# Loads, statistics and three operations in another order at the seams of a time-mixing stage

## The reference, cut to what matters

```
xn  = layernorm(x);  sx = shift(xn) - xn                      # previous row, the state's for the first
xxx = tanh((xn + sx * maa_x) @ maa_w1);  five corrections = xxx_j @ maa_w2_j
x5_j = xn + sx * (maa_stack_j + correction_j)                 # decay, key, value, receptance, gate
w = exp(-exp(time_decay + tanh(x5_w @ decay_w1) @ decay_w2))
r, k, v = x5_r @ Wr.T, x5_k @ Wk.T, x5_v @ Wv.T;  g = silu(x5_g @ Wg.T)
s <- k v + w * s  for each of 128 rows, out = r . (u * k v + s)   # a 16 x 16 state for each of 32 heads
x = x + (groupnorm(out) * g) @ Wo.T
```

## Time and profile before

| | |
|---|---|
| median of three runs | 3070.8 us |
| the profiled execution | 3071.39 us, its span 3069.6 us |
| time mixing ends, channel mixing begins (first instruction of DVE) | 751.41 us |
| PE, DVE, ACT, POOL busy, share of the span | 94%, 58%, 38%, 17% |
| granted TensorE clock, mean | 0.973 |

### The profile page before, as it was taken

One profiled execution on the slowest core, in us unless ns is written; L12 is line 12 of the kernel. 1 busy time (PEld: TensorE's weight loads), 2 busy tenths in 40 slices (PEclk: granted clock), 3 DMA queues, 4 the chain that ended last, 5 costly groups with the idle time before them and its releaser, 6 DMA issues.

```text
span 3069.6 us, 41094 instructions
## 1 busy us (share of the span) xinstructions
PE 2881.2 (94%) x14864; PEld 2179.8 (71%) x14864; DVE 1779.6 (58%) x2615; ACT 1163.7 (38%) x2537; POOL 534.8 (17%) x375
## 2 busy tenths in 40 slices
PE   5988889896897999999999999999999999999899
PEld 2333333332776888888888878888888888888787
DVE  5988979796866444455444464454444554444644
ACT  3232323221534343434434343354434453433432
POOL 2856747483001000001000010010000000000100
PEclk8989999997998999999999999999999999999999
DMA  5001010102124111110111112121110111111011
GB/s 159 1 13 43 1 56 0 42 0 73 67 80 159 55 38 55 38 55 32 38 55 38 55 35 62 41 90 38 55 38 31 55 39 55 38 49 33 22 55 55
DMA packets 54779, 148.71 MB, mean 48 GB/s; under 512 B 6256, under 2 KB 7536, under 8 KB 53584
## 3 DMA queue, kind: packets, MB, share of 16 engines
q1 hardware_dynamic: 51824, 143.80, 14.1%
q0 software_dynamic: 2880, 3.94, 0.6%
HBM read 131.20 MB, written 12.58 MB: 47 GB/s over the span
## 4 chain that ended last, share of the span: by engine, by line
PE 67%; DVE 2%; ACT 1%; issue 0%; DMA 0%; ACTq 0%; DVEq 0%
PE ca_ps L60 19%; PE ca_ps L62 19%; PE ca_ps L61 19%; PE ca_ps L1954 4%; PE ca_ps L1938 4%; PE ca_ps L1946 2%; PE ca_ps L1980 1%; DVE ca_stats L68 0%; DVE ca_xres L1715 0%; DVE ca_ctx_lo L1746 0%; DMA ca_xres<-in_ctxT 0%; DVE ca_wq_lo L1673 0%; ACT ca_sk L1631 0%; DVE ca_h_lo L1740 0%; ACT L1631 0%
## 5 line engine op out<-in xcount | busy, mean ns | idle before, releaser
L1715 DVE TENSOR_TENSOR ca_xres<-ca_xres,ca_ps 128x512 f32<-128x512 f32 x384 | 264.1, 688 | 243.8 <-PE ca_ps L62 238.9
L1502 ACT ACTIVATE ca_pr<-ca_ps,ca_nb 128x129 f32<-128x129 f32 x512 | 181.8, 368 | 511.0 <-DVE ca_nb L1698 510.9
L60 PE MATMUL ca_ps<-ca_h_hi,ca_wq_hi 128*128 128x512 f32 x768 | 312.7, 407 | 4.7 <-DVE ca_h_lo L1740 4.2
L609 DVE TENSOR_TENSOR_SCAN tm_xn<-tm_wd,tm_vb 128x512 f32<-128x512 f32 x256 | 298.5, 1208 | 12.0 <-POOL tm_xf L316 3.5
L62 PE MATMUL ca_ps<-ca_h_hi,ca_wq_lo 128*128 128x512 f32 x768 | 302.6, 394 | 0.0
L61 PE MATMUL ca_ps<-ca_h_lo,ca_wq_hi 128*128 128x512 f32 x768 | 300.6, 391 | 0.0
L60 PE MATMUL ca_ps<-ca_wv_hi,ca_ctx_hi 128*128 128x256 f32 x1024 | 298.0, 291 | 0.0
L62 PE MATMUL ca_ps<-ca_wv_hi,ca_ctx_lo 128*128 128x256 f32 x1024 | 287.6, 281 | 0.0
L61 PE MATMUL ca_ps<-ca_wv_lo,ca_ctx_hi 128*128 128x256 f32 x1024 | 287.3, 281 | 0.0
L1455 POOL TENSOR_TENSOR ca_dv<-ca_bvr 128x256 f32<-128x256 f32 x32 | 23.8, 745 | 1453.9 <-DVE ca_v L1683 1443.8
L60 PE MATMUL ca_ps<-ca_wo_hi,ca_ct_hi 128*128 128x512 f32 x640 | 253.5, 396 | 0.2 <-DVE ca_xres L1715 0.2
(11 more groups left out here) (232 smaller groups left out, 5799.6 us busy)
## 6 DMA issues: line engine op xcount, KB each, us to landing
ca_sq<-in_wq SPq DMA_DIRECT2D x49, 512.0 KB, 5.2
ca_so<-in_wo SPq DMA_DIRECT2D x48, 512.0 KB, 3.5
ca_sk<-in_wk SPq DMA_DIRECT2D x33, 512.0 KB, 6.5
ca_sv<-in_wv SPq DMA_DIRECT2D x32, 512.0 KB, 3.7
ca_bvr<-in_bvb SPq DMA_DIRECT2D x32, 256.0 KB, 3.9
tm_xq<-in_x SPq DMA_DIRECT2D x16, 256.0 KB, 4.5
tm_xres<-in_x SPq DMA_DIRECT2D x4, 1024.0 KB, 6.1
x_dram<-tm_xres SPq DMA_DIRECT2D x4, 1024.0 KB, 4.7
```

The costliest lines, as they stand in the source:

```text
L60: pe.matmul(out, lhs[0], rhs[0], start=first, stop=False)
L609: v.tensor_tensor_scan(state[t % 2][:, d, :], wd[:, g].rearrange("p b t -> p (b t)"), pair[:, d, :], 0.0, ALU.mult, ALU.add).then_inc(scan ...
L1502: ins = act.activation(pr[hd][:, b, :], ps[:, BANK_SC + b // 2, o:o + KW], ACT.Exp, bias=nbs[hd][:, b:b + 1], scale=SCALE, accum_out=sms[h ...
L1715: v.tensor_tensor(xres[U.h][:, U.quad * 4 + b, :], xres[U.h][:, U.quad * 4 + b, :], ps[:, BANK_O + b % 2, :], ALU.add).then_inc(o_out, 1)
```

## The change

- **SP.** The loop is written out. The rows of quad q + 2 and the states of quad q + 1 are requested in the turn of quad q, after its `xres` and ahead of the wait for `res_added`. Quad 1's rows are still requested at the start.
- **DVE, statistics.** `norm_stats` and `norm_gather` for quads 2 and 3 go from between the mixes of `body(1)` and `body(2)` into `joint(0)` and `joint(1)`: two ahead of `gated(q, 2)`, two and the gather behind `inverse(q, 3)`. Quad 1's stay in `body(0)`.
- **DVE, wait.** The wait for PE's last accumulation (`rs_used`) moves from ahead of `shift` to behind its first small copy.
- **DVE, mix.** `mix(q + 1, 1, 0)` goes ahead of `hidden_lo_last`.
- **DVE, loop.** Quads 1 and 2 are written out instead of looped.
- **ACT.** `gate_mix(1)` goes ahead of `decay(2)`.
- **PE.** `value(0)` waits for `decay_out` 5 instead of 8: for `decay(2)` to have read its bank, not for all decays.

```diff
@@ SP
+            load_states(0)
+            ... (wk, wr)
+            load_rows(1)
+            ... (wg, wo)
+            for q in range(NQ):
                 sp.wait_ge(x2_out, q * 16 + 16)
                 sp.dma_start(xres[:], ...).then_inc(res_in, 16)
+                if q < NQ - 2:
+                    load_rows(q + 2)          # waits for xn0_ready, (q + 2) * 4
+                if q < NQ - 1:
+                    load_states(q + 1)        # waits for s0_set, (q + 1) * STEPS
                 sp.wait_ge(res_added, q * 4 + 4)
                 sp.dma_start(x2[...], xres[:]).then_inc(x2_out, 16)
-            quad(0, True, False)
-            with sp.Fori(1, NQ - 1) as q:
-                quad(q, False, False)
-            quad(NQ - 1, False, True)
@@ ACT body
                 gate_mix(0)
+                gate_mix(1)
                 decay(2)
                 decay(3)
-                gate_mix(1)
@@ DVE shift
                 v.wait_ge(sx_ready, q * 5 + 1)
+                if q > 0:
+                    v.wait_ge(rs_used, q * STEPS)
@@ DVE body
                     mix(q, 4, c, first)
-                    if not last:
+                    if first:
                         norm_stats(q + 1, c)
-                if not last:
+                if first:
                     norm_gather(q + 1)
@@ DVE joint
+                more = q + 2 < NQ
+                if more:
+                    norm_stats(q + 2, 0)
+                    norm_stats(q + 2, 1)
                 gated(q, 2)
                 v.wait_ge(rs_ready, q * STEPS + STEPS)
-                v.wait_ge(rs_used, q * STEPS + STEPS)
                 shift(q + 1)
                 inverse(q, 3)
+                if more:
+                    norm_stats(q + 2, 2)
+                    norm_stats(q + 2, 3)
+                    norm_gather(q + 2)
                 hidden_lo(q + 1)
                 gated(q, 3)
+                mix(q + 1, 1, 0)
                 hidden_lo_last(q + 1)
-                mixes(q + 1, 1)
+                for c in range(1, EC):
+                    mix(q + 1, 1, c)
@@ DVE
-            with v.Fori(1, NQ - 1) as q:
+            for q in range(1, NQ - 1):
                 body(q, False)
                 joint(q)
@@ PE value
-                            pe.wait_ge(decay_out, q * 8 + 8)
+                            pe.wait_ge(decay_out, q * 8 + 5)
```

More of the change, by code:

```diff
@@ L220, in _, with load_rows, load_states @@
                 sp.dma_start(tile[:], io[name]).then_inc(const_in, 16)
-            def quad(q, first, last):
-                if not first:
+            def load_rows(q):
+                sp.wait_ge(xn0_ready, q * 4)
+                for b in range(4):
+                    load_x(q, b)
+            def load_states(q):
+                if q > 0:
                     sp.wait_ge(s0_set, q * STEPS)
                 sp.dma_start(s0[:], io["s0"][bass.ds(q, 1)].rearrange("a p c d b -> (a p) c d b")).then_inc(s0_in, 16)
-                if first:
-                    sp.dma_start(wk[:], io["l0w"][1]).then_inc(wkr_in, 16)
-                    sp.dma_start(wr[:], io["l0w"][2]).then_inc(wkr_in, 16)
-                if not last:
[L230 to L235, removed]
+            load_states(0)
+            sp.dma_start(wk[:], io["l0w"][1]).then_inc(wkr_in, 16)
+            sp.dma_start(wr[:], io["l0w"][2]).then_inc(wkr_in, 16)
+            load_rows(1)
+            sp.dma_start(wg[:], io["l0w"][3]).then_inc(late_in, 16)
+            sp.dma_start(wo[:], io["l0w"][4]).then_inc(late_in, 16)
+            for q in range(NQ):
                 sp.wait_ge(x2_out, q * 16 + 16)
                 sp.dma_start(xres[:], io["x"][bass.ds(q * 4, 4)].rearrange("b t e -> t b e")).then_inc(res_in, 16)
+                if q < NQ - 2:
+                    load_rows(q + 2)
+                if q < NQ - 1:
+                    load_states(q + 1)
                 sp.wait_ge(res_added, q * 4 + 4)
                 sp.dma_start(x2[bass.ds(q * 4, 4)].rearrange("b t e -> t b e"), xres[:]).then_inc(x2_out, 16)
-            quad(0, True, False)
-            with sp.Fori(1, NQ - 1) as q:
-                quad(q, False, False)
-            quad(NQ - 1, False, True)
             sp.wait_ge(x2_out, NQ * 16 + 16)
```

## The result

The changed kernel takes 3050.9 us (median of four executions, 3048.88 to 3053.72) against 3069.84 for the kernel before; the ratio is 0.9943, with a 95% interval of 0.9930 to 0.9955. On record was 3051.5, between 3045 and 3060. The profiled execution took 3048.88, with a span of 3047.1: 22.5 less than the span of 3069.6. It is the fastest of the four, and the profile before (3071.39) lies near that kernel's slowest; the medians differ by 19.0. What follows explains the 22.5.

The account below looks back on a forecast made before the run. DVE's instructions bound time mixing's steps, chained waits its joints, PE the rest. Gains of 21.2 less 0.9 and 0.3, plus 1.5 for a vanished low stretch, minus 1.5 for clock: 20.0 off 3071.4; forecast 3051.5 us, range 3045 to 3060.

Parts of the forecast that it names:

- Part 1: First two joints: rows requested early and statistics moved into DVE's waits, at no cost there; gain 10.8 us.
- Part 2: gate_mix(1) ahead of decay(2) ends PE's stop ahead of mix(5, 2): 6.5 us over three joints, 3.0 in the opening.
- The 1.5 of the vanished low stretch: First joint: low clock following PE's stop ahead of mix(5, 2) should go with the stop, gaining 1.5 us.
- Part 3: mix(1, 0) ahead of hidden_lo_last, where DVE waits for ACT's copy: 0.3 us a joint, 0.9 in all.
- Part 4: Wait for rs_used behind shift's copy: 0, since the slowed subtraction would end with POOL's addition anyway; otherwise 0.9 us.
- Part 5: DVE's quads 1 and 2 written out: steps lose 0.9 us, double waits in two joints 0.3.
- Part 6: PE's low clock may fall inside any joint: 1.5 us lost, bounds -3.1 (first spared) and +6.2 (both others hit).
- the order moves the stop only: Rival: PE's stop moves to mix(3, 3) or mix(4, 0), gaining 2 or 3 instead of 11; 3060 us, chance 0.09.
- the stall stays: Rival: receptance(0) again runs at low clock, so DVE's wait for POOL's first product stays; 3055 us, chance 0.07.
- The clock lands in both later joints: Rival: the low clock falls into the second and third joints; 3056 us, chance 0.17.
- Better than I say: Rival: the first joint is spared the low clock as well; 3047 us, chance 0.12.
- slower: Rival: low clock settles in the dense steps, each microsecond costing up to 0.8; some 3080 us, chance 0.02.

Follow-up runs that it names:

- b_gate: Kernel before with one part alone, ScalarE's gate_mix(1) ahead of decay(2): 3064.45 us against 3068.27, ratio 0.9989.
- u_gate: Changed kernel with ScalarE's gate_mix(1) back behind decay(3): 3065.04 us.
- u_decay: Changed kernel with value(0) waiting for all eight decay outputs again: 3055.15 us.
- u_rs: Changed kernel with DVE's wait for rs_used back ahead of the copy that opens shift: 3049.6 us.
- c_loop: Changed kernel with DVE's quads 1 and 2 in a loop again, and statistics taken once more that nothing reads: 3050.32 us.
- m_first: Changed kernel with DVE's wait for rs_ready moved from the scan to the product ahead of it: 3052.76 us.
- b_loads: Kernel before with SyncE's new order alone (rows and states requested early): 3069.02 us against 3069.48, ratio 1.0000.
- w_warm: Changed kernel with four throwaway TensorE products, one at each of t = 27 to 30 of every quad: 3048.76 us.
- w_fill: Changed kernel with six throwaway TensorE products in every quad, two at t = 26, one at each of t = 27 to 30: 3048.66 us.
- c_both: Changed kernel with DVE's quads 1 and 2 looped again and six throwaway TensorE products (t = 26 to 30) in every quad: 3049.99 us.

## Why the prediction was right, step by step

The mechanisms of parts 1 and 2, which make most of the gain, came out as told; that the total was off by only 0.6 is in part luck. The 20.0 was taken off the profile's 3071.4 although that is 0.6 above the median; off the median it gives 3050.8. Between the medians the gain was 19.0, 1.0 less than 20.0, and between the profiles, to which the terms below add up, 22.5, 2.5 more. Single terms were off by up to 2.3, in both directions.

- **Part 1, 10.8: right.** 11.05 - 5.96 = 5.09 and 11.71 - 5.96 = 5.75, 10.84. By the runs the early rows are 2.5 + 3.2 and the statistics 2.4 each, 10.5 of the 10.8. "Both are covered, the first by 0.1 only" held.
- **Part 2, 6.5 in the joints and 3.0 in the opening: right in mechanism, small in size.** b_gate and u_gate give 2.4 a joint, 7.3 in all, instead of 2.15. The opening gave 2.15 in this profile; the nine profiles' average of 71.1 against 72.99 and 74.28 with the old opening is 2.5. Without the relaxed wait the two profiles there are (u_decay 74.19, b_gate 73.65) show no gain, where I had 1.2; with it but without the new order (u_gate, 74.36) there is none either.
- **The 1.5 of the vanished low stretch: right**, with 1.5 in u_gate.
- **Part 3, 0.9: failed.** "I take 0.3 a joint": it is 0. I looked at what DVE waited for at that place, and not at the next waits for TensorE behind it, which take up any gain.
- **Part 4, 0: failed.** "An earlier start ends at the same moment": it ended 0.23 earlier a joint, 0.7 in all, and 0.20 more in the two looped ones, which were written out. The Trainium skill (GPSIMD Engine Reference, Key points) does say that the two engines contend, and the trace agrees: the subtraction took 1.76 instead of 0.69 beside the addition. But that the slowed subtraction hangs on GpSimd's end was my own inference, and it was wrong.
- **Part 5, 0.9 + 0.3 lost: right in size by luck.** The steps lost 0.39 + 0.84 = 1.2. 0.36 of it is a stop of 0.46 at L582 in quad 2, behind DVE's own L578, that u_rs, with the wait elsewhere, doesn't have (118.48); its cause is open. The 0.3 that I took off for double waits in two joints was wrong in sign: they gained 0.20 each. The second wait costs the 2.0 a quad that I worked out (c_loop, m_first). The reason I gave for the stall was wrong: b_loads keeps the statistics between the mixes and has no stall, so it was the late rows'.
- **Part 6, 1.5 lost: the place was wrong, the bounds held.** The first joint was spared, which gives 3.1, and the second was hit, which takes 2.3: a gain of 0.8, 2.3 better than my term and the largest miss of the sum. Other profiles of kernels with the same joints have others hit (0 and 2 in u_decay, 1 and 2 in w_warm), so this term was luck either way. The Trainium skill (TensorE: Matmul & The Clock Gate, What's actually happening) has the chip's look at activity run freely; that the hit moves from joint to joint in the table with small shifts of length, and that w_fill's second joint is hit and its third not behind the same instructions, agrees.

Joint by joint it closes. The third: 2.4 + 0.23 + 0.20 = 2.83, measured 2.85. The second: 5.75 + 2.83 - 2.3 = 6.3, measured 6.25. The first: 5.09 + 2.4 + 0.23 + 4.8 for a hit in the old order that is gone = 12.5, measured 12.50.

Of the rivals, "the statistics are not hidden", "the order moves the stop only" and "the stall stays" are refuted by the spared joints and by steps in which no scan waits for GpSimd. "The clock lands in both later joints" did not come true here, where one was hit, but did in w_warm. "Better than I say" came true in half, and was paid for in the next joint. The price in "slower" was too high: a microsecond at half clock leaves at most half a microsecond of work undone, not 0.8, so that case needed still more low clock than the 34 us there. Nor did 14 us at a mean clock of 0.54 at the end of the steps lose anything (w_fill).

## What to carry to other kernels

Compare stages, and first sort them by the clock at their start: b_loads removed 9.2 us of waits and measured 0, and in its profile the low clock lies in two more joints, at 4.8 each. A stop of TensorE costs its length (2.4 here) and, at times, 1.5 more behind it in clock; taking away the stop (the order on ScalarE) was the part that also made a hit cheaper. And before crediting a moved operation, follow it to the next wait on the same engine, which may take up the gain (`mix(1, 0)`) or pass it on (the shift).

## What was not expected of the hardware

- GpSimd's addition of 128x512 took 1.39, 1.62 or 1.83 us, depending on when DVE's subtraction beside it began, while that took 1.76 each time.
- A jump back in DVE's loop cost 4.93 and 4.95 us in two kernels (c_loop, c_both) and nothing in others whose loop has as many instructions.
- A second wait cost DVE 0.07 us ahead of a scan that follows its product, and nothing when it stood ahead of the product (product to product 3.49 instead of 3.56).
- Half the clock in TensorE's thin last steps cost nothing there: their last 14 us went at a mean clock of 0.54 or of 1.00, and the steps took 118.5 either way.
